# A four-stage network on one core: the sampling table in two copies instead of four, statistics by batch, and other joints between the stages

## What is computed

```
x = x + L0(gn(x))   # 1x1 conv, offsets by a 1x1 conv, bilinear samples at 9 taps, summed with weights per channel and tap
x = x + L1(gn(x))   # involution: 49 weights per pixel and channel from a reduced map (batch-normalised, relu)
x = x + L2(gn(x))   # deformable 3x3 conv: offsets and a sigmoid mask by a 3x3 conv, bilinear samples, 9 x 128 x 128 weights
x = x + L3(gn(x))   # attention over the 2304 pixels of a batch, 8 heads of 16 channels, softmax, output projection
```

```
out = out + g * (wgt * valid)[:, None]     # over yi in (y0, y0+1), xi in (x0, x0+1)
wgt = (1 - |y - yi|) * (1 - |x - xi|)      # pixels outside of the map count as zero
```

## Time and profile before

| what | value |
|---|---|
| median of 3 runs | 2274.11 us (2273.6 to 2276.54) |
| profiled execution, its time | 2275.15 us |
| its span, first to last instruction | 2273.3 us |
| PE busy | 1771.8 us (78%) |
| DVE busy | 1743.7 us (77%) |
| ACT busy | 1131.7 us (50%) |
| POOL busy | 1161.6 us (51%) |
| mean granted TensorE clock | 0.878 |

### The profile page before, as it was taken

The page is one execution under the profiler, slowest core; times in us unless marked ns, Lnnn a source line. Parts: engine busy times, 40 slices in busy tenths (PEclk is TensorE's granted clock), DMA queues, the critical chain, the costliest instruction groups (busy, mean ns, idle before and its releaser), DMA issues.

```text
span 2273.3 us, 36261 instructions
## 1 busy us (share of the span) xinstructions
PE 1771.8 (78%) x12204; PEld 1001.7 (44%) x12204; DVE 1743.7 (77%) x4324; ACT 1131.7 (50%) x2887; POOL 1161.6 (51%) x1282
## 2 busy tenths in 40 slices
PE   4344444468888876444489999999999999999998
PEld 2344444435454543344345555555534444444433
DVE  3777777769999984777488888878867888888871
ACT  2333333320000002333328888888777777777776
POOL 2777777726666663777577777777241000000000
PEclk9666666769999998766669999999999999999999
DMA  7877777710000009777443443443102111110101
GB/s 235 271 206 205 206 207 205 207 33 1 1 1 1 1 10 284 206 206 207 120 92 102 120 110 97 107 105 106 19 1 35 26 24 22 27 22 18 24 1 43
DMA packets 111257, 222.62 MB, mean 98 GB/s; under 512 B 18784, under 2 KB 63968, under 8 KB 110816
## 3 DMA queue, kind: packets, MB, share of 16 engines
q0 software_dynamic: 51840, 169.91, 25.7%
q1 hardware_dynamic: 59232, 50.40, 9.8%
HBM read 174.62 MB, written 24.38 MB: 88 GB/s over the span
## 4 chain that ended last, share of the span: by engine, by line
PE 43%; ACT 4%; issue 2%; DVE 2%; SPq 0%; DMA 0%; POOL 0%; ACTq 0%
PE ps L1328 13%; PE ps L1292 13%; PE ps L1306 11%; ACT l_e L1053 3%; PE ps L1385 2%; PE ps L1375 1%; PE ps L1313 1%; ACT corner L1027 1%; DVE l_mx L1174 1%; PE ps L1339 1%; PE ps L1345 0%; PE ps L1366 0%; PE ps L1352 0%; DVE l_rest L1162 0%; ACT l_part L1080 0%
## 5 line engine op out<-in xcount | busy, mean ns | idle before, releaser
L1174 DVE TENSOR_REDUCE l_mx<-ps 128x1 f32<-128x384 f32 x1728 | 835.0, 548 | 137.7 <-PE ps L1306 137.4
L1053 ACT ACTIVATE l_e<-ps 128x384 f32<-128x384 f32 x1728 | 724.3, 511 | 219.1 <-PE ps L1292 217.3
L1306 PE MATMUL ps<-l_ka,l_qs 96*128 96x384 bf16 x1728 | 571.7, 334 | 11.3 <-DMA l_qs<-l_part 6.1
L1292 PE MATMUL ps<-l_qs,l_ks 99*128 99x384 bf16 x1728 | 566.2, 331 | 10.3 <-ACT l_e L1053 4.5
L468 PE MATMUL ps<-c_ident,l_samp 128*128 128x128 f32 x486 | 116.8, 424 | 358.5 <-DVE l_samp L385 358.5
L225 POOL DMA_INDIRECT l_corner<-table,l_idx x324 | 314.8, 972 | 141.0 <-issue 97.9
L385 DVE SCALAR_TENSOR_TENSOR l_samp<-l_corner,l_wts,l_samp 128x128 f32<-128x128 f32 x972 | 285.3, 349 | 120.6 <-ACT l_samp L305 112.7
L1328 PE MATMUL ps<-l_e,l_v_s 128*32 128x384 f32 x3456 | 332.4, 493 | 1.6 <-ACT l_e L1053 0.8
L614 DVE SCALAR_TENSOR_TENSOR l_prod<-ps,c_b,l_pad 128x384 f32<-128x384 f32 x588 | 312.3, 608 | 25.1 <-PE ps L649 25.1
L1292 PEld LDWEIGHTS ps<-l_qs,l_ks 99*128 99x128 bf16 x1728 | 166.5, 97 | 368.9 <-ACT l_e L1053 194.7
L550 POOL TENSOR_TENSOR l_prod<-l_prod 128x1152 f32<-128x1152 f32 x84 | 221.3, 2635 | 141.0 <-DVE l_prod L614 141.0
(11 more groups left out here) (158 smaller groups left out, 1919.4 us busy)
## 6 DMA issues: line engine op xcount, KB each, us to landing
table<-l_tok SPq DMA_DIRECT2D x32, 640.0 KB, 7.6
l_ka<-l_part SPq DMA_DIRECT2D x96, 72.0 KB
l_ks<-l_part SPq DMA_DIRECT2D x96, 72.0 KB, 2.7
l_corner<-table,l_idx POOLq DMA_INDIRECT x324, 3.7
l_qs<-l_part SPq DMA_DIRECT2D x96, 48.0 KB
corner<-table,idx POOLq DMA_INDIRECT x270, 3.7
x_map<-in_x SPq DMA_DIRECT2D x2, 1152.0 KB, 6.5
l_qs<-l_part SPq DMA_DIRECT2D x96, 24.0 KB
```

The costliest lines, as they stand in the source:

```text
L1053: nc.scalar.activation(e[:, w % 2, i, :], ps[:, st_bank(at), 0:QC], ACT.Exp).then_inc(s["st_free"], 1)
L1174: nc.vector.tensor_reduce(mx[:, ga % MAX_SLOTS, u // NQC, u % NQC:u % NQC + 1], ps[:, ab_bank(at), 0:CH], AX.X, ALU.max) \
L1292: nc.tensor.matmul(ps[:, bank, 0:QC], ks[:, head % 2, kt * 128:(kt + 1) * 128], qs[:, gb % 3, j * QC:(j + 1) * QC], start=True, stop=True) \
L1306: nc.tensor.matmul(ps[:, bank, 0:CH], qs[0:KROWS, ga // CT % 3, q0:q0 + 128], ka[:, head % 2, k0:k0 + CH], start=True, stop=True).then_inc ...
```

## The change

Six things are done.

1. **Table of two copies.** A table row is 256 floats: the pixel and the one PW rows on. A gather reads 512 floats from the start of a row on, so it spans two rows. The corners come as (0, PW, 1, PW + 1), and the weights are written in that order. The index counts floats now (times 256).
2. **Statistics by batch** in both sampling blocks: the first batch is normalised before the second has its statistics; TensorE and ScalarE have their part of the second behind the tokens of the first. x of the first batch is loaded in two halves, and ScalarE does one root of a constant at the very start. The sigmoid's early use moves behind the second root.
3. **Order of turn and combine**: `combine(i - 1)` stands ahead of `turn(i)`.
4. **Second batch's first calls** go from L2's block into attention: six gathers ahead of the splits on GpSimd, three behind them, nine in beats. Sample 0 is prepared in beats; `FIRST_BEAT` goes from 2 to 5, and `NORM_AT`, `PROJ_AT`, `VALUES_AT` from 84, 88, 94 to 86, 90, 97.
5. **Splits spread over engines**: on entry ScalarE writes the second part, in a ring of three remainders; in the windows VectorE takes the first part off, a window after the projection, and GpSimd does the other two. The memset of `ks` goes from GpSimd to VectorE.
6. Second batch in attention: its normalisation in six pieces, `take_v` of head 8 at window 106, and SP's waits for the splits in three steps.

```diff
-CORNERS = (0, 1, PW, PW + 1)
+COPIES = (0, PW)
+TWIDE = len(COPIES) * 128
-BEATS, FIRST_BEAT = 5, 2
-NORM_AT, PROJ_AT, VALUES_AT, LOAD_AT = 84, 88, 94, 10
+BEATS, FIRST_BEAT = 5, 5
+NORM_AT, PROJ_AT, VALUES_AT, LOAD_AT = 86, 90, 97, 10
+def norm_vector_of(nc, dve, chain, s, t, b, write, loaded):
+    for q in range(NCH):
+        if q in loaded:
+            dve.wait_ge(loaded[q], 16)
+        last = nc.vector.bn_stats(t["bst"][:, b, q, :], t["x"][:, b * S + q * CH:b * S + (q + 1) * CH])
...
+    dve.wait_ge(s["means"], b + 1)
...
+    dve.wait_ge(s["std"], b + 1)
+    chain.link(nc.vector.reciprocal(t["rstd"][:, b:b + 1], t["std"][:, b:b + 1]))
+    write(b, t["gm"][:, b, 0:1], t["rstd"][:, b:b + 1]).then_inc(s["norm"], 1)
...
+        from_row = [tb.rearrange("r (c one) -> (r c) one", one=1) for tb in table]
...
-                            corners[slot][:, k, :], None, table[b],
+                            corners[slot][:, k, :], None, from_row[b],
...
-                for i in range(TILES + 2 if modulated else ALL_TILES):
+                for i in range(tiles):
...
-                    for j, d in enumerate(CORNERS):
+                    for j, d in enumerate(COPIES):
...
+                    nc.scalar.activation(early[:, :], g["eps"][:, 0:1], ACT.Sqrt)
...
-                    for j, (wy, wx) in enumerate(((gt, gt), (gt, fr), (fr, gt), (fr, fr))):
+                    for j, (wy, wx) in enumerate(((gt, gt), (fr, gt), (gt, fr), (fr, fr))):
...
-                                                   float(GUARD + PW + 1), None, ALU.add)
+                                                   float(GUARD + PW + 1), float(TWIDE), ALU.add, ALU.mult)
...
+                    if b == 0:
+                        norm_tensor_of(nc, pe, s, t, 1)
...
                 for i in range(tiles + 1):
+                    if i >= 1:
+                        combine(i - 1)
                     if i < tiles:
                         turn(i)
-                    if i >= 1:
-                        combine(i - 1)
...
+                for gr in range(GROUPS - 1):
+                    fetch(0, gr)
+                for n in range(HALF):
+                    side, cols = part_of(n)
+                    pool.wait_ge(s["part3"], n + 1)
+                    nc.gpsimd.tensor_tensor(part[:, side, 2, cols], rest[:, n % RESTS, :], part[:, side, 1, cols],
+                                            ALU.subtract).then_inc(s["split"], 1)
+                fetch(0, GROUPS - 1)
...
-                weigh_second(0)
-                weigh_corner(0, 2)
-                chain.link(add_corner(0, 1, 2))
...
-                for m in range(2 * K2):
-                    scale_corner(0, m)
...
+                    if n:
+                        side, cols = part_of(n - 1)
+                        act.wait_ge(s["part2"], n)
+                        nc.scalar.copy(part[:, side, 1, cols], rest[:, (n - 1) % RESTS, :]).then_inc(s["part3"], 1)
...
+                nc.vector.memset(ks[KROWS:KROWS + MROWS, :, :], 1.0).then_inc(s["ones"], 1)
...
-                    nc.vector.tensor_copy(part[:, side, 1, cols], rest[:, n % 2, :]).then_inc(s["part2"], 1)
...
+                def less_first(n):
+                    side, cols = part_of(n)
+                    dve.wait_ge(s["st_free"], no.st["proj", n] + 1)
+                    y = rest[:, n % RESTS, :]
+                    nc.vector.tensor_tensor(y, y, part[:, side, 0, cols], ALU.subtract).then_inc(s["less"], 1)
...
+                        if w == NORM_AT + 3 and j < NCH:
+                            if j == 0:
+                                invert(1)
+                            normalised(1, j, j + 1)
+                        if j in (1, 3) and j // 2 < len(proj_of(w - 1)):
+                            less_first(proj_of(w - 1)[j // 2])
...
+    for b, q in ((0, 0), (0, half)):
+        sp.dma_start(g["x"][:, q * CH:(q + half) * CH], g["in_x"][b, :, q * CH:(q + half) * CH]) \
+            .then_inc(g["x_loaded"][b][q], 16)
```

More of the change, by code:

```diff
@@ L113, with norm_vector @@
 GN_SEMS = "stats means var std norm gchain "
-def norm_vector(nc, dve, s, t, write, stats=None, loaded=None):
+def norm_vector(nc, dve, s, t, write, stats):
     chain = Chain(dve, s["gchain"])
-    if stats is None:
-        stats = NCH
-        for b in range(B):
-            if loaded:
-                dve.wait_ge(loaded[b], 16)
-            for q in range(NCH):
-                last = nc.vector.bn_stats(t["bst"][:, b, q, :], t["x"][:, b * S + q * CH:b * S + (q + 1) * CH])
-        chain.link(last)
     for b in range(B):
@@ L202, in sampling_layer @@
             xg = sb("xg", [128, N])
-        gap = turned[0:GUARD, 0, 0:4 * 128]
+            early = sb("early", [128, 1])
+        gap = turned[0:GUARD, 0, 0:TWIDE]
         taps = K2 if modulated else 1
-        table = [nc.dram_tensor(f"table{2 * modulated}_{b}", [TROWS, 4 * 128], F32).ap() for b in range(B)]
+        table = [nc.dram_tensor(f"table{2 * modulated}_{b}", [TROWS, TWIDE], F32).ap() for b in range(B)]
+        from_row = [tb.rearrange("r (c one) -> (r c) one", one=1) for tb in table]
         if modulated:
-            g["table2"] = table[1]
+            g["table2"] = from_row[1]
         tiles = TILES if modulated else ALL_TILES
@@ L334, in write @@
                                                        mean, rstd, ALU.subtract, ALU.mult)
-                norm_vector(nc, dve, s, t, write, loaded=None if modulated else g["x_loaded"])
+                gn = Chain(dve, s["gchain"])
+                for b in range(B):
+                    norm_vector_of(nc, dve, gn, s, t, b, write, {} if modulated else g["x_loaded"][b])
                 if not modulated:
@@ L782, in attention_layer @@
         part = sb("part", [128, 2, 3, S], BF16)
[L783 removed]
+        rest = sb("rest", [128, RESTS, CH])
         v_all = sb("v_all", [128, NH, KT, HD])
@@ L884, in _ @@
                         sp.wait_ge(s["st_full"], no.st["score", gb * WPB - 1, 2 * CT - 1] + 1)
+                        if gb == LOAD_AT:
+                            sp.wait_ge(s["split"], HALF + NCH + CT)
+                        if gb == LOAD_AT + 1:
+                            sp.wait_ge(s["split"], 2 * HALF)
                         queries(gb + 2)
@@ L960, in split_parts @@
                     side, cols = part_of(n)
-                    pool.wait_ge(s["st_free"], no.st["proj", n] + 1)
-                    y = rest[:, n % 2, :]
-                    p0, p1, p2 = (part[:, side, i, cols] for i in range(3))
-                    chain.link(nc.gpsimd.tensor_tensor(y, y, p0, ALU.subtract))
+                    pool.wait_ge(s["less"], n - HALF + 1)
+                    y = rest[:, n % RESTS, :]
+                    p1, p2 = (part[:, side, i, cols] for i in range(1, 3))
                     chain.link(nc.gpsimd.tensor_copy(p1, y))
```

127 lines of the change are left out of this document (73 added, 54 removed).

## The result

The changed kernel took **2242.78 us** (median of four runs, 2241.57 to 2244.84) against 2274.02 before: 0.986 of it, 95% interval 0.9848 to 0.9872, 31.2 us faster. The forecast was 2240.5, range 2234 to 2249. The profiled execution took 2243.17 with a span of 2241.3, so the two spans differ by 32.0 where the sum said 33.6.

What follows compares the result with a forecast made beforehand. Attention was taken as bound by TensorE, each sampling stage as paced by GpSimd issuing gathers. Seven terms sum to 33.6 us off the profiled 2275.15, giving 2241.55, or 2240.5 at the median; range 2234 to 2249.

Steps and rivals of the forecast that it cites:

- Opening: Start to first gather: halved table writes, beginning earlier, let the first gather go 12.2 us earlier; bounds 10 to 13.5.
- Ends of the sampling stages: Combination ahead of the last turn saves some 0.5 us at each of two stages, 1.0 in all; bounds 0 and 2.
- Entry of the second stage: Second sampling stage's first gather waits for the index; six of twelve statistics leave the path: 2.5 us, bounds 1.5 and 3.3.
- Joint: Second sampling to attention: without 18 gathers GpSimd's drain ends under TensorE's tail, attention starts 15.3 us earlier; bounds 14.5 and 15.6.
- Rival 3: Joint with attention: the drain's tail is a fixed price of leaving the block, 7.4 us remain, 2248; chance 0.05.
- Entry of attention: Start of attention to TensorE's start: splits at some 1.06 us each, tenth split ends 1.2 us earlier; bounds -1 and 3.
- Beats: Attention's warm stretch saves copies, sums and idleness; later beats return 3.6 us in the windows: net 0.9, bounds -2 and 2.5.
- middle: Middle of attention: normalisation in six pieces spares a TensorE wait, head 8 queries may wait: 0.5 us, bounds -1.5 and 2.
- Rival 1: Sampling stages: gathers over two rows cost more to issue or land; 2368 at the slowest gather's cost; chance 0.03.
- rival 2: Warm stretch: GpSimd late at the first turning, TensorE waits, some 5 us, 2245.5; chance 0.15.
- rival 4: Index, not table, starts the first gathers, and head 8 queries come late: 4 us, 2244.5; chance 0.1.
- rival 5: Entry of attention: TensorE may stay at full clock with under 2 us idle: some 4 us more gained, 2236.5; chance 0.12.

Runs made afterwards that it cites:

- the gathers in the block: Changed kernel with the 18 gathers of the second batch's samples 0 and 1 back in the second sampling stage's block, none in attention; 2256.97 us.
- three gathers ahead: Changed kernel with memset behind remainders, turn first, first queries from two queues, and only three gathers ahead of subtractions, six behind those queries' landing; 2242.96 us.

## Why the prediction was right, and where it was not

The sum came out at 32.0 against 33.6 because its three large terms held; small ones erred both ways, and that they nearly cancelled is luck. So is the distance of the total, 2.3 us: the same program took 2245.64 when it was run again, 5.1 above the forecast and still inside the range.

- **Opening (12.2): 12.0.** Averaging when the constants land, table as the last wait: right. The copies are worth 9.6 of it (9.3 forecast), the earlier start of the table writes 2.4 (3.0 forecast). The experiment with all statistics together puts 1.1 to 2.5 us on the statistics by batch; the rest (table load, halved first load) was not taken apart.
- **Ends of the sampling stages (1.0): about -0.6**, all of it at the second; of the 1.0 lost between first gather and next block at the first, half lies inside the stage, whose gathers took 410.6 to 413.1 us over all profiles. The step that failed is "now the first (2.65) runs while VectorE still sums and holds up the turn by about 0.9". I read 5.29 for two combinations as 2.65 each. At half clock one takes 4.21, and the clock is at half there, in a stage where TensorE has little to do. It held the turn up by 2.3 us (sum ended 1078.14, turn 1080.46) for the 2 or so it saved behind. The earlier trace rows showed the pair where more than half of it already ran at full clock: the granted clock of its 5.29 us was 0.78.
- **Entry of the second stage (2.5): 3.2**, and 3.3 taken away by the experiment; my upper bound.
- **Joint (15.3): 15.3**, shown by the experiment that puts the gathers back. Rival 3 fell.
- **Entry of attention (1.2): 0.2.** The split pace was better than forecast (0.88, not 1.06), and two things took it back: the memset, whose duration was right (3.93 forecast, 3.90) but which began 0.8 us later than I had it (5.1 behind the start, not 4.3; the row has 1.01 us of idleness ahead of it), so that the first split stood at 10.2 instead of 9.4; and "behind it the loads take 5.3 us as before". They took 6.8, because I had put three gathers beside them in the change's description and not in the sum. Both causes were removed one by one, for 1.4 to 1.7 us each. Before's second profile had an entry of 27.2, so the gain of 0.2 could as well be read as 1.0.
- **Beats (0.9) and middle (0.5): 2.2 in the profiled pair**, tail included, of which the clock made most. Over ten profiles with the changed warm stretch (all but those with the gathers in the block and with three gathers ahead) it lasted 54.6 on the mean (53.6 to 56.4), before 57.3 in two: 2.7 gained, not the 4.45 of the forecast, and uncertain by a good part of that, for equal code differs by up to 2.8. Windows give back 0.56 up to the 81st and 1.94 in the middle (137.51 against 135.57, neither with a fall of the clock), 2.5 in all instead of 3.6: the windows of the middle were no clean 4.47 before either. Pieces: 0 instead of 0.5 to 1.5.

Rival 1 fell with the pace; rival 2 was near (0.8 us of wait for the mixed corners, and 4.1 for GpSimd in all once it was delayed further); rival 4 was not seen, the queries of head 8 cost 0.4 us; rival 5 had the clock the wrong way: though the idle 15.6 us were gone, the first projections still ran at half (the granted clock was 0.52 from 1089 to 1096 us). One sign of being wrong was badly drawn: a wait of over 3 us for `l_qs` stood in the kernel before already (6.06) and stands in the changed one (8.99), at the first by-query matmul.

## What to carry to other kernels

Gaps at the joints are worth more than work inside a stage: 27 of 32 us came from two waits that ended with a transfer or a barrier. What is moved ahead to fill a gap must be priced at the clock that rules there, and against what it now delays; and transfers moved beside a short, waited-for load lengthen it, so they belong behind its landing. When two profiles differ by 1 to 3 us, profile the same kernel twice before naming a cause, and measure a stretch from its own first instruction: counted from the start of the kernel the two copies seemed worth 8.5 us, from the first table write it is 9.6 in every profile.

## What was unexpected

Six loads of 48 KB that land in 5.3 to 5.4 us alone need 6.75 to 7.1 beside three gathers of 256 KB. TensorE's clock falls from full to half once after the warm stretch, in one of two places, at a cost of 1.1 to 1.5 us. In the middle of the warm stretch it ran at 0.50 for 17 to 31 us without a break (31 in the changed kernel's first profile, where the records of TensorE and VectorE are both 95% busy in that time). Issuing from a second queue brought nothing for these loads.
